# A new order of steps in the main loop of a gated-delta-rule layer, and two more slots ahead of its loop

## The reference

```
q, k, v = silu(causal_conv4(x @ w_q)), ... ; q, k = l2norm(q), l2norm(k)
beta = 2*sigmoid(x @ w_b);  g = -exp(A_log)*softplus(x @ w_a + dt_bias)
for t:                                   # one state S (64 x 128) per head
    S = S*exp(g_t);  delta = (v_t - k_t@S)*beta_t
    S = S + outer(k_t, delta);  o_t = (q_t/8) @ S
y = rmsnorm(o) * norm_w * silu(x @ w_g);  out = y @ w_out
```

## Time and profile before

| | |
|---|---|
| time, median of 3 (lowest, highest) | 5079.9 us (5079.02, 5081.31) |
| profiled execution, its own time | 5079.9 us |
| its span | 5078.7 us |
| PE busy | 4849.3 us, 95% |
| DVE, ACT, POOL busy | 4096.7 (81%), 3391.6 (67%), 3099.6 us (61%) |
| mean granted PE clock | 0.981 of full speed |

### The profile page before, as it was taken

The page is one execution under the profiler, slowest core; times in us unless marked ns, Lnnn a source line. Parts: engine busy times, 40 slices in busy tenths (PEclk is TensorE's granted clock), DMA queues, the critical chain, the costliest instruction groups (busy, mean ns, idle before and its releaser), DMA issues. The chain is left out here.

```text
span 5078.7 us, 151121 instructions
## 1 busy us (share of the span) xinstructions
PE 4849.3 (95%) x44460; PEld 3853.0 (76%) x44460; DVE 4096.7 (81%) x9991; ACT 3391.6 (67%) x10245; POOL 3099.6 (61%) x4445
## 2 busy tenths in 40 slices
PE   6699999999999999999999999999999999999788
PEld 6377777777777777777777777777777777777566
DVE  5588888888888888888888888888888888886675
ACT  1477776767677676776776767767677677676453
POOL 3566666666666666666666666666666666665565
PEclk9899999999999999999999999999999999999788
DMA  4101011011110111101101111011010110100110
GB/s 149 67 34 40 32 45 40 31 39 37 40 38 31 39 40 37 38 31 43 42 31 38 35 44 38 31 39 44 33 38 31 39 46 31 38 32 19 57 51 34
DMA packets 116468, 208.27 MB, mean 41 GB/s; under 512 B 12418, under 2 KB 70932, under 8 KB 116372
## 3 DMA queue, kind: packets, MB, share of 16 engines
q1 hardware_dynamic: 116372, 207.10, 11.9%
HBM read 187.66 MB, written 19.40 MB: 41 GB/s over the span
## 5 line engine op out<-in xcount | busy, mean ns | idle before, releaser
L648 DVE SCALAR_TENSOR_TENSOR cv<-ps_a,wqkv,cv 128x511 f32<-128x511 f32 (+2 forms) x1536 | 1139.2, 742 | 221.4 <-ACT cv L641 220.9
L633 PE MATMUL ps_a<-xin,wqkv 128*128 128x512 f32 x2048 | 997.3, 610 | 31.1 <-POOL m L1116 31.1
L852 POOL TENSOR_TENSOR bm<-bat,mask 128x256 f16<-128x256 f32 x1536 | 1023.8, 691 | 0.0
L1055 POOL TENSOR_TENSOR rms<-msq,epsq 128x2 f32<-128x2 f32 x512 | 99.6, 194 | 1387.5 <-ACT sqo L1050 1387.5
L913 DVE TENSOR_TENSOR tt<-tt,b 128x256 f16<-128x256 f16 x1536 | 624.9, 414 | 189.4 <-PE b L908 188.6
L955 ACT CAST tt<-bu 128x256 f16<-128x256 f32 x1536 | 576.2, 375 | 205.9 <-PE bu L950 199.3
L902 ACT ACTIVATE m<-b 128x256 f16<-128x256 f32 x1536 | 574.0, 391 | 32.5 <-PE b L897 32.2
L633 PEld LDWEIGHTS ps_a<-xin,wqkv 128*128 128x128 f32 x2048 | 350.5, 191 | 279.5 <-issue 279.4
L1087 PE MATMUL ps_a<-wout,yT 128*128 128x256 f32 x2048 | 559.2, 396 | 0.5 <-ACT yT L1081 0.5
L780 PE MATMUL ps_b<-wgate,xin 128*128 128x256 f32 x2048 | 503.0, 388 | 0.3 <-DVE ktok L709 0.3
L908 PEld LDWEIGHTS b<-m,tt 128*128 128x128 f16 x6144 | 339.1, 98 | 215.8 <-issue 183.1
(11 more groups left out here) (223 smaller groups left out, 12579.8 us busy)
## 6 DMA issues: line engine op xcount, KB each, us to landing
xin<-xT_scratch SPq DMA_DIRECT2D x128, 512.0 KB, 3.3
grow<-g_scratch SPq DMA_DIRECT2D x128, 512.0 KB, 4.1
gam<-g_scratch SPq DMA_DIRECT2D x256, 96.0 KB, 2.9
n_x<-in_x SPq DMA_DIRECT2D x16, 512.0 KB, 3.5
xT_scratch<-n_xT SPq DMA_DIRECT2D x16, 512.0 KB, 2.6
e_x<-in_x SPq DMA_DIRECT2D x16, 512.0 KB, 4.2
out_y<-e_yo SPq DMA_DIRECT2D x16, 512.0 KB, 2.9
wqkv<-in_w_qkv SPq DMA_DIRECT2D x32, 128.0 KB, 3.3
```

What stands on the lines that cost most here:

```text
L633: ins = pe.matmul(ps[:], wqkv[:, k, j * P:(j + 1) * P], xin[p][:, k, :], start=k == 0, stop=k == KT - 1)
L648: s.done(dve.scalar_tensor_tensor(y[:, r:], ps[:, 0:T - r], tap[:, j, TAPS - 1 - r:TAPS - r], y[:, r:], ALU.mult, ALU.add), f"a_tap{j}{r}")
L852: s.done(pool.tensor_tensor(half_of(bm[:, l, units(g), :], l, 1), half_of(bt[:, units(g), :], l, 1), half_of(c["mask"][:, l, :].unsqueeze( ...
```

## The change

The table `SLOT_ORDER` is replaced by another one of the same 223 steps, in another order and with other cuts between slots: `a_proj2` and `a_proj3` are done in the item's slot 0 and no longer in slot 1, the recurrence's `c_O1`, `c_KS2`, `c_Z2` in slot 2 and no longer in slot 3. The highest lag stays 3. And 12 slots are written out ahead of the loop where it was 10.

```diff
 SLOT_ORDER = """
-    b_n0.1 b_Me01.2 a_tanh0.1 a_silu0.1 b_M20.2 c_O1.3 b_V01.2 b_Ve01.2 b_Me20.2 b_ss.1 c_sq1.3 b_Ue10.2 a_proj3.1
...
+    b_kT.1 b_V40.2 b_U11.2 a_tap32.1 b_Ve11.2 c_yTe1.3 c_SU2.3 a_tap33.1 b_bm31.2 b_sq0.1 c_O2.3 b_Ve40.2 b_M21.2
+    b_n0.1 b_Ue11.2 b_bm41.2 c_S2.3 a_tanh3.1 b_U40.2 a_silu3.1 b_lo0.2 b_M50.2 b_Me21.2 b_Me50.2 b_Ue40.2 c_sq2.3
...
@@ phase_delta
-        in_slots(nc, NIT, LAGS, 10, COMPUTE, body)
+        in_slots(nc, NIT, LAGS, 12, COMPUTE, body)
```

More of the change, by code:

```diff
@@ L68 @@
-    b_vT0.1 c_out3.3 c_R1.2 a_tap01 b_t21.1 c_Z1.2 b_vtok0.1 b_Ue00.1 b_bm01.1 b_hi0.1 a_tap02 b_Tq1.1 b_V10.1
-    c_u1.2 b_Tf1.1 b_Ve10.1 a_tap03 c_yT0.2 b_U10.1 b_kT b_bm11.1 c_SU1.2 c_yTe0.2 b_sel b_sq0 b_M01.1 c_acc3.3
+    b_kT.1 b_V40.2 b_U11.2 a_tap32.1 b_Ve11.2 c_yTe1.3 c_SU2.3 a_tap33.1 b_bm31.2 b_sq0.1 c_O2.3 b_Ve40.2 b_M21.2
+    b_n0.1 b_Ue11.2 b_bm41.2 c_S2.3 a_tanh3.1 b_U40.2 a_silu3.1 b_lo0.2 b_M50.2 b_Me21.2 b_Me50.2 b_Ue40.2 c_sq2.3
+    b_V21.2 c_KS3.3 c_m2.3 b_U21.2 b_ss.1 b_Ve21.2 b_V50.2 c_out1.3 c_R3.3 b_Ue21.2 b_Ve50.2 c_p2.3 b_M31.2 c_Z3.3
@@ new lines @@
+    b_U50.2 c_acc0.3 c_acc1.3 b_rc.1 b_P0.2 c_y2.3 b_kk0.1 b_gam.1 c_u3.3 b_w1.1 b_R0.2 b_kw.1 b_ktok.1 c_yT2.3
+    b_Ue50.2 b_Me31.2 b_ev00.1 b_V31.2 b_Ve31.2 b_ev01.1 b_F0.2 b_bm51.2 c_yTe2.3 b_U31.2 b_Ue31.2 b_root.1 b_qT.1
+    b_eps.2 b_sq1.1 c_O3.3 c_sq3.3 c_out2.3 c_acc2.3 b_diag0.1 c_m3.3 b_t20.1 c_p3.3 b_kk1.1 b_M41.2 b_T0.2 b_n1.1
+    c_Z0.2 b_Me41.2 b_vT0.1 b_bm00.1 c_u0.2 b_ev10.1 b_Tq0.1 b_U41.2 b_hi0.1 b_V41.2 b_Ue41.2 b_vtok0.1 a_proj0
+    c_y3.3 b_Tf0.1 b_Ve41.2 b_M00.1 b_M51.2 c_yT3.3 b_ev11.1 b_vT1.1 b_vtok1.1 b_bm10.1 b_Me00.1 c_SU0.2 b_V00.1
@@ new lines @@
+    b_U00.1 b_Ve00.1 b_Me51.2 c_yTe3.3 b_V51.2 c_out3.3 c_O0.2 b_Ve51.2 c_S0.2 b_Ue00.1 b_M10.1 a_cv0 b_P1.2
+    b_U51.2 c_sq0.2 b_Ue51.2 c_acc3.3 c_KS1.2 a_tap01 b_Me10.1 a_proj1 b_gend.1 b_R1.2 b_F1.2 a_tap02 b_V10.1
+    c_R1.2 b_sel c_m0.2 c_p0.2 b_U10.1 a_tap03 b_E0 b_diag1.1 a_cv1 c_y0.2 a_tanh0 b_g0.1 b_Ue10.1 b_t21.1 c_Z1.2
+    c_yT0.2 b_T1.2 b_bm20.1 b_Ve10.1 a_tap11 a_silu0 a_tap12 b_tg0.1 b_Tq1.1 b_M20.1 b_bm01.1 c_u1.2 b_bm30.1
+    a_tap13 a_proj2 b_Tf1.1 b_Me20.1 b_U20.1 b_kqs.1 b_sg0.1 a_tanh1 a_silu1 c_yTe0.2 b_V20.1 c_SU1.2 a_cv2 b_M01.1
@@ L70 @@
+    b_Ue20.1 b_bm40.1 c_O1.2 b_Ve20.1 a_tap21 a_tap22 b_M30.1 b_Me01.1 c_S1.2 b_E1 b_g1.1 b_bm50.1 b_V01.1 b_Me30.1
+    a_tap23 c_sq1.2 b_Ve01.1 b_U30.1 b_tg1.1 b_V30.1 b_Ve30.1 c_m1.2 a_tanh2 b_bm11.1 a_proj3 b_hi1.1 b_M40.1
+    b_Ue30.1 c_p1.2 c_KS2.2 b_sg1.1 a_silu2 a_cv3 c_y1.2 c_R2.2 b_Me40.1 b_M11.1 b_U01.1 b_Ue01.1 c_out0.2 c_Z2.2
+    c_yT1.2 b_lo1.1 b_Me11.1 b_V11.1 a_tap31 c_u2.2 b_bm21.1
 """.split()
```

## The result

The changed kernel takes 5165.05 us (5162.3 to 5168.27), the kernel before in the same runs 5080.6 us: ratio 1.0167, 95% interval 1.0149 to 1.0184. It is 1.7% slower. The forecast was 5158 us, with a range of 5120 to 5208; the measured time is 7 us above the forecast.

The account below looks back on a forecast made before the run. PE was taken to bound the kernel, busy 2073.38 of 2100 us in the body. Slots +69, grow tile +10, loop -0.6, filling and draining 0: total +78 us on 5079.9, so 5158 us, with a range of 5120 to 5208.

Parts of the forecast that it names:

- The new wait at the second `b_kk`: PE waits there for DVE's `c_acc2` to read the bank `c_out2` has just filled: +0.92 us a slot.
- The turning point at 0.29 us: Length of the wait at the second `b_kk` below which the changed kernel would be faster than before.
- the faster rival: Second `b_kk` doesn't wait because `c_acc2` is through in time: slot 34.37 us, total 5045 us; chance 0.08.
- The new wait at `b_V21`: PE waits there for `b_Me21` on ACT, which needs `b_M21`: +0.41 us a slot, bounds 0.38 and 0.8.
- The old wait at `c_SU2`: PE's wait for ACT's copy `c_u2` goes, as five steps now stand ahead: -0.43 us a slot with small waits.
- The borders: Fewer PE changes from f16 to f32 steps, 0.08 us each, some 0.05 or 0.10: -0.34 us a slot.
- rival 3: Borders between f16 and f32 steps cost nothing, so their gain doesn't come: 35.63 us a slot, 5200 us; chance 0.04.
- The slot: Sum of the terms for one written-out slot: 34.73 to 35.29 us, +0.56, or +69 us for 124 slots.
- The grow tile: Its load comes late seven times, PE held at `b_Tq1` and `b_M20`: 3.1 us instead of 1.7, +10 us in all.
- The loop: 58 iterations instead of 59, each costing 0.60 us more than two written-out slots: -0.6 us.
- Filling and draining: Three slots' worth of PE work at the kernel's ends, unpriced for the new order: 0, with -8 and +8.
- rival 1: More waits than the two, as late ACT or DVE steps hold those behind: 0.3 us a slot more, 5195 us; chance 0.15.

Follow-up runs that it names:

- experiment 1: Changed kernel with `c_out2` put ahead of `c_O3`, whose matmuls then stand between `c_out2` and the second `b_kk`: 5083.86 us, ratio to before 1.0007.
- experiment 2: Kernel before with `c_out2` and `c_acc2` put directly ahead of the second `b_kk`, all else in the old order: 5196.82 us, ratio 1.0233.
- Experiment 3: Changed kernel with `b_M21` put ahead of `c_O2`: 5169.77 us, ratio 1.0177.
- Experiment 5: Kernel before with five steps moved so that three f32 steps alone between f16 steps get an f32 neighbour: 5070.23 us, ratio 0.9981.
- experiment 9: Kernel before with 42 slots written out ahead of the loop in place of 10: 5137.58 us, ratio 1.0112.
- experiment 7: Changed kernel with `c_out2` ahead of `c_O3`, grow load ahead of `wo`, `b_kT` behind `b_M50`, `b_sq0` and `b_n0` later: 5107.18 us, ratio 1.0052.
- experiment 8: Kernel of experiment 7 with `b_n0` and `b_ss` moved on DVE: behind `c_acc1` 5101.89 us, ratio 1.0042; behind `b_Ve50` 5055.15 us, ratio 0.995.

## Why the prediction was right, point by point

- *The new wait at the second `b_kk`*, +0.92 forecast: 0.88 measured per written-out slot and 0.99 in the loop, 104.0 us in the list for 126 of them against "some 90". In the written-out slots `c_acc2` started 0.20 us behind `c_out2`'s streaming, in the loop 0.33, where I had 0.39 from rows of the loop; it took 0.42, and 0.25 us passed from its end to `b_kk` where I had 0.15. The two errors nearly cancel, so the near hit is partly luck. The 0.10 by which the second hand-over was too small may be the price of `b_kk` itself, which I had counted as gone because `c_out2` is f32; experiment 1 points that way. Experiments 1 and 2 take it out and put it in. The turning point at 0.29 us was far off, and with it the faster rival.
- *The new wait at `b_V21`*, +0.41: 0.41. What was to be hidden behind it, `c_KS3`, comes 0.01 us late in the written-out slots and 0.08 in the loop. Experiment 3 shows how near the two are.
- *The old wait at `c_SU2`*, -0.43: 29.7 us of waits became 0.3. Gone, as said.
- *The borders*, -0.34: some -0.26 measured in the written-out slots, step by step from starts of PE's rows. The four behind 128-wide steps gave 0.22 and the one at `b_kk` 0.09, as priced; `c_yT2`, which now stands behind `b_kk0`, costs 0.06 more, a change from one f32 step to another that I had not priced. This is the term that was most too large. Experiment 5 tells the price apart: 0.08 us each, as in the earlier trace rows. By the Trainium skill (TensorE: Matmul & The Clock Gate, Part 2, "Step-by-step: what each phase is for") the next weights load while this matmul runs, and by that alone a border would be free; here it isn't, the measurement decides, and rival 3 falls.
- *The slot*: 35.29 forecast, 35.38 measured: 0.08 of it is the borders, 0.05 the small waits beside the old one, 0.01 `c_KS3`, less 0.05 at `b_kk`. 124 x 0.09 is 11 us, more than the 7 that were missing; the loop took 9 back.
- *The grow tile*, +10: seven slots are longer by 3.5 us in the mean, where it was 1.7, so +12.7; I had 3.1. The time was nearly right and the way partly wrong. PE was held not at `b_M20` but at `c_yT0`, by way of `c_p0` and `c_y0`, and at `b_Tq1`, by way of ACT; and POOL waited 9.2 us in the mean and not 5, since it arrives at `b_sel` earlier. In three of the seven the clock comes on top (below).
- *The loop*, -0.6: -9. An iteration costs 0.45 us instead of 0.60. I had priced only the one iteration that goes, and taken the price of the rest as fixed; experiment 9 shows how little fixed it is. Nor is it the same cost: before it lay ahead of `c_O1` (0.45 us) and of `b_M20` (0.14), and these two have gone. Now 0.12 us in each slot is the longer wait at the second `b_kk`, 0.07 is `c_KS3`, and some 0.07 in each iteration is `c_out1`. That this term and the slot's err in opposite directions is why the total lies closer than its parts.
- *Filling and draining*, 0: -2.7 us (span +81.8 less 84.5).
- *More waits than the two* (rival 1): in the changed kernel only the small ones at `c_KS3` and `c_out1`, nearly all of them in the loop. In experiments 1, 5, 7 and 8 they do appear, each time a part goes faster or is moved.

The sum as measured: 124 x 0.655 = 81.2, +12.7, -9.2, -2.7: +82 of the profiled spans' difference of 81.8.

## What to carry to other kernels

When an order of steps is judged, look first for an instruction that reuses a buffer right behind its last writer: that is writer, reader, writer in a chain with two hand-overs between engines, here 0.87 to 1.0 us each time, however idle the reader is; 0.88 us of other work in between left 0.1 of it. A step moved to cover one wait must be followed on every engine that it touches: most of the moves tried here gave back all or most of their gain at a step that stood behind one of the moved ones, on DVE or on PE. And a per-iteration cost read from a loop holds for that loop's code alone; a wait priced from rows of the loop can be another in written-out code, here by 0.12 us.
